# A four-layer gated cross-attention and mixture-of-experts kernel: fetched rows are added, measured and normalised in small pieces at other steps, and the last layer ends with six of its shared blocks

## The reference

```python
for l in range(4):
    x = x + tanh(g_xattn[l]) * attention[l](layernorm(x), ctx)
    x = x + tanh(g_ffn[l])   * moe[l](layernorm(x))
```

```python
p = softmax(x @ router_w);  top_p, top_i = top_k(p, 2)
y = gelu(x @ shared_up) @ shared_down + x
y += sum over the 2 chosen e of top_p[e] * (gelu(x @ routed_up[e]) @ routed_down[e])   # 256 -> 1024 -> 256
```

## Time and profile before

| | us |
|---|---|
| median of 3 runs (lowest, highest) | 3227.09 (3226.1, 3247.94) |
| profiled execution | 3231.42 |
| its span | 3229.6 |
| PE busy | 2621.8 (81%) |
| DVE busy | 1581.4 (49%) |
| ACT busy | 1262.4 (39%) |
| POOL busy | 1254.6 (39%) |

### The profile page before, as it was taken

One profiled execution on the slowest core, in us unless ns is written; L12 is line 12 of the kernel. 1 busy time (PEld: TensorE's weight loads), 2 busy tenths in 40 slices (PEclk: granted clock), 3 DMA queues, 4 the chain that ended last, 5 costly groups with the idle time before them and its releaser, 6 DMA issues. The chain is left out here.

```text
span 3229.6 us, 56174 instructions
## 1 busy us (share of the span) xinstructions
PE 2621.8 (81%) x18096; PEld 2400.5 (74%) x18096; DVE 1581.4 (49%) x3623; ACT 1262.4 (39%) x3098; POOL 1254.6 (39%) x1213
## 2 busy tenths in 40 slices
PE   4674479389979999879992689996899897899993
PEld 4574378389968888769992578885788887888882
DVE  3665555366635444346642234434677676343232
ACT  3232134144443333225442334443666565433331
POOL 0012461665322845032205457502544543174313
PEclk9786689698979999969985789998999999899996
DMA  3031244211011533111002234310000000042212
GB/s 113 1 131 47 83 156 132 60 41 34 18 30 47 147 95 112 43 41 34 28 2 62 86 110 135 109 40 30 21 20 13 20 13 27 1 141 89 93 59 88
DMA packets 127510, 205.89 MB, mean 64 GB/s; under 512 B 16401, under 2 KB 88365, under 8 KB 127137
## 3 DMA queue, kind: packets, MB, share of 16 engines
q1 hardware_dynamic: 63232, 117.84, 12.0%
q10 hardware_dynamic: 50208, 47.31, 4.6%
q0 software_dynamic: 13824, 37.53, 3.6%
HBM read 145.58 MB, written 57.02 MB: 63 GB/s over the span
## 5 line engine op out<-in xcount | busy, mean ns | idle before, releaser
L503 ACT ACTIVATE moe_act<-moe_gu 128x256 f32<-128x256 f32 (+1 forms) x431 | 189.3, 439 | 619.2 <-PE moe_gu L95 619.0
L93 PE MATMUL moe_gu<-moe_whi,moe_xThi 128*128 (+2 forms) x1018 | 411.6, 404 | 10.4 <-POOL moe_wlo L294 10.4
L93 PE MATMUL moe_yp<-moe_whi,moe_hThi 128*128 (+1 forms) x1238 | 392.7, 317 | 8.1 <-DVE moe_hTlo L788 7.7
L95 PE MATMUL moe_gu<-moe_whi,moe_xTlo 128*128 (+2 forms) x1018 | 391.7, 385 | 0.0
L94 PE MATMUL moe_gu<-moe_wlo,moe_xThi 128*128 (+2 forms) x1018 | 390.6, 384 | 0.0
L294 POOL TENSOR_TENSOR moe_wlo<-moe_raw,moe_whi 128x768 fp32r<-128x768 f32 (+1 forms) x170 | 341.1, 2007 | 37.2 <-issue 13.8
L94 PE MATMUL moe_yp<-moe_wlo,moe_hThi 128*128 (+1 forms) x1238 | 349.9, 283 | 0.0
L95 PE MATMUL moe_yp<-moe_whi,moe_hTlo 128*128 (+1 forms) x1238 | 349.3, 282 | 0.0
L788 DVE TENSOR_TENSOR moe_hTlo<-moe_tp,moe_hThi 128x256 fp32r<-128x256 f32 (+1 forms) x431 | 210.6, 489 | 238.8 <-ACT moe_hThi L509 237.6
L772 DVE TENSOR_TENSOR moe_h<-moe_act,moe_gu 128x256 f32<-128x256 f32 x321 | 135.0, 420 | 373.5 <-ACT moe_act L503 358.6
L292 POOL CAST moe_whi<-moe_raw 128x768 fp32r<-128x768 f32 (+1 forms) x170 | 152.2, 896 | 300.7 <-DMA moe_raw<-in_moe_w 300.6
(11 more groups left out here) (463 smaller groups left out, 6900.5 us busy)
## 6 DMA issues: line engine op xcount, KB each, us to landing
moe_raw<-in_moe_w SPq DMA_DIRECT2D x118, 384.0 KB, 3.2
moe_raw<-in_moe_w SPq DMA_DIRECT2D x52, 512.0 KB, 4.2
moe_xr<-rows_x ACTq DMA_DIRECT2D x69, 256.0 KB, 2.8
rows_y<-moe_y ACTq DMA_DIRECT2D x69, 256.0 KB, 2.2
rows_x<-att_zeros SPq DMA_DIRECT2D x16, 512.0 KB, 6.7
att_cT_hi<-ctxT_hi SPq DMA_DIRECT2D x24, 256.0 KB, 2.8
att_cT_lo<-ctxT_lo SPq DMA_DIRECT2D x24, 256.0 KB, 3.0
moe_xr<-rows_x ACTq DMA_DIRECT2D x41, 128.0 KB, 2.0
```

Of the source, the lines that this page charges most:

```text
L93: pe.matmul(out, lhs[0], rhs[0], start=first, stop=False, **kw)
L95: return pe.matmul(out, lhs[1], rhs[0], start=False, stop=last, **kw)
L503: act.activation(act_sb[i % 2][:, :], gu[i % 2][:, 0:HC], func).then_inc(act_done, 1)
```

## The change

Three functions change; the arithmetic on each number stays the same, apart from the order in which terms are added to `x`.

1. `small_phase`: `take_rows` becomes pieces (K pieces of two adds, "stats", "means"), emitted at different steps. POOL's work at the start is reordered: `dg` and `dgc` become two DVE instructions (24 POOL instructions before), `QT[0]` is cleared by DVE, fetch(1) moves behind norm(0), and `add_bias(b)` comes before the batch's residual (which now waits for it) and no longer waits for it. k, v and kT of batch 0 come a few steps earlier.
2. `wide_phase`: pieces of take_rows(i + 2) at h = 6, 12, 14, 15; roots at h = 0, norm in two parts at h = 1 and 2, fetch at h = 3 and 4, add_bias(i) at h = 9. The first batch is normalised by DVE.
3. `moe_phase` with LATE = 6 in layer 3: 10 shared blocks, 39 routed, 6 shared, for which the shared weights are loaded and split again. The last store of `rows_y` and the gathers are issued by POOL behind the last split; their rows have 8 buffers of their own, and DVE adds them after the late blocks. Each batch is stored to `out` when it is complete; `final_phase` is gone. PER is 8 (was 3); the inputs of block 10 are turned half a block later, the loads of routed rows are issued at step 18 (was 28).

```diff
--- before.py, after.py: moe_phase
+    SE = SJ - LATE
...
-        mask_step = shift_step + 2 + (n_mask - 1) // PER if PER else -1
+        mask_step = shift_step + 1 + (n_mask - 1) // PER if PER else -1
...
+        def gathered_by(b):
+            return max(0, min(T, 3 * (b - RE + 1) - 5)) if b >= RE else 0
...
+                if out is not None:
+                    for b in range(B):
+                        sp.wait_ge(x_final, TB * b + TB)
+                        sp.dma_start(out[b].rearrange("(t p) d -> p t d", p=P), x[:, TB * b:TB * b + TB, :]).then_inc(out_stored, 16)
...
+                if LATE:
+                    at, q = loads[-1]
+                    a = (at - SE) * P
+                    pool.wait_ge(y_copied, NB)
+                    pool.dma_start(rows_y[a:ROWS, :].rearrange("(t p) d -> p t d", p=P), y_sb[q % 2][:, 0:RE - at, :]).then_inc(y_last, 16)
+                    pool.wait_ge(y_last, 16)
...
+                        for t in range(gathered_by(done - 1), gathered_by(done)):
+                            add_rows(t)
--- wide_phase
+        TAKE = dict(zip((*((6, 12) if K == 2 else (6, 8, 12)), 14, 15), PIECES))
...
-                        if h == 1 and not last:
-                            take_rows(i + 1)
+                        if h in TAKE and i < B - 2:
+                            take_rows(i + 2, TAKE[h])
...
-                        if h == 1 and i < B - 1:
-                            roots(i + 1)
-                            norm(i + 1)
-                        if h == 8 and i < B - 2:
-                            fetch(i + 2)
-                        if h == 9 and i > 0:
-                            add_bias(i - 1)
-                add_bias(B - 1)
+                        if i < B - 1:
+                            if h == 0:
+                                roots(i + 1, 0)
+                                roots(i + 1, 1)
+                            if h in (1, 2):
+                                norm(i + 1, 2 * h - 2)
+                                norm(i + 1, 2 * h - 1)
+                        if i < B - 2 and h in (3, 4):
+                            fetch(i + 2, h - 3)
+                        if h == 9:
+                            add_bias(i)
--- small_phase
-    TAKE = [-27, -11, *(16 * (b - 1) - 20 for b in range(2, B))]
+    TAKE = {}
+    for b in range(B):
+        for piece, off in zip([*range(K), "stats", "means"], (*((-21, -19) if K == 2 else (-22, -21, -19)), -16, -16)):
+            at = (-29, -11)[b] if b < 2 else 16 * (b - 1) + off
+            TAKE.setdefault(at, []).append((b, piece))
...
+                    if rotary and s == -10:
+                        v.tensor_tensor(dg[:, :, :, :].rearrange("p b t k -> p (b t) k"), ident[:, :].rearrange("p (o k) -> p o k", o=1).broadcast_to([P, B * TB, P]),
+                                        flat(kq).rearrange("p (n o) -> p n o", o=1).broadcast_to([P, B * TB, P]), ALU.mult)
```

More of the change, by code:

```diff
@@ L137, in moe_phase @@
     NJ = SJ + NB
+    RE = SE + NB
     NR = NB
+    NX = NE + bool(LATE)
     ROWS = NR * BS
@@ L149, in moe_phase @@
     NI = NJ * NG
-    NGA = 8
+    NGA = 4 if LATE and glu else 8
     UE = NG * NS
@@ L1408, in _ @@
                 for pos, (kind, part) in enumerate(FIRST):
+                    if (kind, part) == ("kT", 1):
+                        for piece in PIECES:
+                            take_rows(0, piece)
                     if (kind, part) == ("nT", 0):
-                        take_rows(0)
+                        norm_first()
                     round_(0, 0, 0, pos, kind, part)
+                    if kind == "qT" and 1 <= part < K + 1:
+                        take_rows(1, part - 1)
                 v.wait_ge(tg_ready, 1)
@@ L1475, in norm, with roots @@
-                def norm(b):
-                    if b == 1:
+                    for k in range(K):
+                        pool.indirect_dma_start(out=gath[:, t, k, :], out_offset=None, in_=G["rows_y"][0:rows, :],
+                                                in_offset=bass.IndirectOffsetOnAxis(ap=G["slot_r"][:, TB * b + t, k:k + 1], axis=0)
+                                                ).then_inc(rows_in, 16)
+                def roots(b, half):
+                    r2 = slice(TB * b, TB * b + TB)
+                    if half == 0:
+                        pool.wait_ge(mv_ready, b + 1)
+                        pool.tensor_scalar(var[:, r2], mv[:, r2, 1], 1e-5, None, ALU.add)
+                        pool.drain()
+                        pool.tensor_tensor(root[:, r2], var[:, r2], minus_half[:, r2], ALU.pow)
+                        pool.drain()
+                        pool.tensor_tensor(var[:, r2], root[:, r2], root[:, r2], ALU.mult)
+                        pool.drain()
+                    else:
+                        pool.tensor_tensor(var[:, r2], var[:, r2], mv[:, r2, 1], ALU.mult)
+                        pool.drain()
+                        pool.tensor_scalar(var[:, r2], var[:, r2], 1e-5, None, ALU.add)
+                        pool.drain()
+                        pool.tensor_tensor(root2[:, r2], var[:, r2], minus_half[:, r2], ALU.pow)
+                        pool.drain()
+                        pool.tensor_tensor(root2[:, r2], root2[:, r2], root[:, r2], ALU.mult)
+                        pool.drain()
@@ L1489, in add_bias @@
                 def add_bias(b):
-                    pool.wait_ge(x_done, b + 1)
-                    pool.tensor_tensor(x_of(b), x_of(b), bc_t(bo[:, :], D), ALU.add)
-                fetch(0)
+                    pool.tensor_tensor(x_of(b), x_of(b), bc_t(bo[:, :], D), ALU.add).then_inc(biased, 1)
+                for t in range(TB):
+                    fetch(0, t)
                 pool.memset(minus_half[:, :], -0.5)
+                pool.drain()
                 pool.memset(QT[0][:, :, :].bitcast(F32), 0.0)
@@ L1496, in _ @@
                 pool.drain().then_inc(cleared, 1)
-                roots(0)
+                roots(0, 0)
+                roots(0, 1)
+                pool.drain().then_inc(root_ready, 1)
+                for t in range(TB):
+                    fetch(1, t)
                 pool.wait_ge(loaded, 64)
-                norm(0)
-                fetch(1)
+                pool.wait_ge(bo_ready, 1)
                 for s in range(LEAD - 1):
@@ L2044, in _ @@
                     turn_in(0, "k")
+                norm(0)
+                pool.wait_ge(kq_done, 1)
+                aux(0, "q")
                 fetch(1)
-                clear(0)
-                pool.drain().then_inc(cleared, 1)
-                if rotary:
-                    for b in range(B):
-                        for t in range(TB):
-                            pool.tensor_scalar(dg[:, b, t, :], ident[:, :], kq[:, b, t:t + 1], None, ALU.mult)
-                    pool.drain()
-                    for b in range(B):
-                        pool.tensor_tensor(dgc[:, b, :], ident[:, :], dg[:, b, 0, :], ALU.subtract)
-                    pool.drain().then_inc(dg_done, 1)
                 norm(1)
+                pool.wait_ge(bo_ready, 1)
+                add_bias(0)
                 for b in range(1, B):
```

343 lines of the change are left out of this document (177 added, 166 removed).

## The result

Over all runs beside each other the kernel before took 3236.26 us (median of 14, 3220.73 to 3248.35) and the changed one 3216.14 us (median of 14, 3205.68 to 3230.99): a ratio of 0.9934, 95% interval 0.9914 to 0.9954. It is faster, by 0.7% where 3.4% were forecast, and lies outside the forecast's range. The profiled execution has a span of 3217.4 us (3229.6 before).

A forecast was written before the change was run, and what follows sets the result against it. PE was taken as the engine on the path, with its holes and the slow clock behind them to win. 27 + 24 + 11 + 2 + 45 = 109 us off the 3229.6 us span gave a forecast of 3118 us, range 3095 to 3145.

The forecast's parts named there:

- Part 1: moe3: the end gains 40 us, the start costs 13, net 27 (17 to 38).
- Part 2: att1: five holes of 2.5 us on DVE's maxima and the slow clock behind them; 80% of 30 taken, gain 24.
- The sign that I named: att1's steady window: a clock of 0.97 or more in the trace after.
- Part 3: Start of att1: norm(1) moves from 628.16 to about 613 to 616 us, gain 11 (5 to 15).
- Part 4: att2: PE 98% busy, no removable hole before the low-clock stretch; gain 2, from -8 to +8.
- what would make the prediction wrong: Whole kernel: the slow clock not being a consequence of holes, or POOL's norm becoming what PE waits for.
- Part 5: att3: gains of 7 and 9 at the start and 29 in the steady part, sum 45 us (34 to 55).
- What there is to win is 25.2 + 7.5: att3 steady: waits on POOL's multiply and `nT_lo`, plus 8 of clock, 40.7 us; 72% taken, 29.
- The one on the slower side: att1 and att2: late norm(b + 1) delays `aux` and PE's qT in 14 batches; 3274 us at 6 us stalls; chance 0.02.
- Within 1%: Whole kernel: time within 32 us of the kernel before; chance 0.03.
- Only the ends pay: Steady stages stay, moe3 gives 27 and the starts 18: 45 us, 3182; chance 0.05.
- 69 us off 3227: Rival that holes only get smaller: att1 12, att3 25, moe3 22, start and att2 10; 3150 us; chance 0.22.

The follow-up runs named there:

- p9: The changed kernel run once more, unchanged: 3216.66 us, ratio 0.9931 to the kernel before.
- p17: Changed kernel with old `small_phase`, att3's residual early, batch adds dealt out and statistics two steps later on DVE: 3307.11 us, ratio 0.9909 to the kernel before.
- p13: The kernel before run again, unchanged, for a second trace: 3343.54 us, ratio 0.9998.
- p8: Changed kernel with `aux` ahead of norm on POOL and att3's residual at the head of step h = 3: 3184.7 us, ratio 0.9816 to the kernel before.
- p10: Changed kernel with 224 extra matmuls on PE in att2, same results: 3227.36 us, ratio 0.9961 to the kernel before.

## Why the prediction was wrong

**Part 1, moe3: right.** Net 27 forecast, 32 measured (29 and 28 in two more traces): the start cost 11.9 us for 13, the end gave 43.6 for 40. The scatter's start, its hole and the second stall each came within 2 us. It was a chain of rows with durations, and the clock hardly moved in it (21.9 and 21.8 us lost).

**Part 2, holes in att1: the step that failed.** It reads "Each of the 5 costs 2.5 us and the clock behind it, 7 us x 0.48 = 3.4". The holes went as forecast, to a single 0.4. But five of 1.4 us, on `att_KT` (DVE's copy of the turned keys), came where the pieces now stand ahead of a copy that PE wants, and three of 2.0 on `aux`. And the clock did not come back with the holes: att1 lost 31.2 before and 42.2 after (44.0 and 40.5 in the other traces of the changed kernel), with 4 to 13 us less idle time. 0.52 for 7 us was read rightly behind holes of 2.5 us, but the loss does not follow the size of the hole: behind the five of 1.4 to 1.5 us in p9 the clock is at half for 7 to 10 us each, in the first trace of the changed kernel behind two of them for 14 and 17. And that it would be full if no hole were there was argued from the windows between; the stretches of 20 us and more without one, in p17 and in p13, the kernel before, show that false. The sign that I named, a clock of 0.97 or more in att1's steady window, came out as 0.89.

**Part 3, the start of att1: mis-sized.** norm(1) was to reach PE at 613 to 616 us, and did at 620.57, behind a hole of 7.03 for 14.50. Two terms were missing. The chain of batch 0 runs 5 us late, with the first wait on `ctx` at 12.42 for 7.39 us: norm(0) begins at 593.95 for 589.31, PE's turn of q at 609.57 for 604.32, and DVE, which adds batch 1 behind that, does so at 609.78 for 607.22. And POOL's first small instruction of norm(1) took 2.09 us at 613.92, against 0.24 elsewhere, beside DVE's `dg` of 2.26. (fetch(1) is not the cause: it stood behind norm(0) in the kernel before too, and starts at 598.79 for 598.07.)

**Part 4, att2: +37 us for -2, of a stage that was thought nearly full.** I gave it -8 to +8 because PE was 98% busy. Of the 37 us 28 are clock and 11 idle time (8.0 at the turn of q, 3.5 at the first wait on `ctx`). The row that should have warned stood in the prediction itself: 17 us at 0.51, with PE's last hole ending 9 us before them. I named it as what would make the prediction wrong, and gave it 8 us either way. It needed more: with PE's work at half clock for 20 to 70 us at a time, an arrangement that moves nothing on PE moved the time by 29 us (p17).

**Part 5, att3: the step "What there is to win is 25.2 + 7.5" failed.** The waits on POOL fell to 7.8 as forecast. One of them, of 3.17 us, lay over a residual that ended 0.6 us before the hole did (2331.37 + 0.74 against 2332.72), so the residual took its place, 14.3 us in all; and behind that, p8 shows, lies POOL again. Of the 8 us of clock 2.3 came. Two waits that end within a microsecond of each other are one wait; a third then takes their place. The start gained: it has nearly all of att3's 10 us, where 16 were forecast for it.

**The rivals.** The one on the slower side had the right mechanism, norm(b + 1) ahead of `aux` ahead of PE's q, and the stall came out as s = 2.0, where 4.4 were needed to turn the sign. It came in 3 batches of att1 and 4 of att2, not in 14, and its holes are 14 us. "Within 1%", chance 0.03, is what happened; of the rivals with a time "Only the ends pay", 3182, chance 0.05, was the nearest, and even it took the new order of the steady stages to be harmless. Two of the prediction's sums don't hold: 69 us off 3227 is 3158, not 3150, and the stall of 6 us is priced against 85 us where its threshold of 4.4 is worked out against 109, which would give 3250 and not 3274. Neither touches the forecast.

## What to carry to other kernels

Split each stage into PE's work at full clock, its holes and the clock's loss before and after a change: the work is constant, so the two others say at once what moved. Where a trace shows a low clock with PE busy and no hole before it, a stage's time is uncertain by that loss whatever is done to the holes, and a sum that counts clock as won with the hole has to be given as a range down to nothing. Before counting a wait as won, look for what else would end within a few microseconds of it, through semaphores that no instruction of the profile stands for.

## What was unexpected of the hardware

- The slow clock without a hole: 21 to 22 us at 0.51 to 0.53, and 74 us at 0.50 at the end of att2, with PE busy for 72 of them. The kernel before has such stretches too. Why an edit on DVE alone (p17) costs clock stays open, and so does why 224 more matmuls (p10) gave 17 of their 27 us back.
- The same kernel on another chip (three of those used) is 3% slower, mostly by idle time in the MoE phases. There the new `small_phase` cost 66 and 64 us; in the first pair of traces, on another chip, att1 and att2 grew by 42.
- A 128x2 instruction of POOL took 2.09 us instead of 0.24 beside a DVE instruction of two inputs, 128x2048, of 2.26 us.
